# A state-space layer and a routed expert layer on one core: one more GpSimd drain ahead of the last four scatters

## The reference

```python
x = hidden_states                                   # (4, 512, 256)
x = x + state_space_block_and_mlp(_layernorm(x))    # 8 heads, chunks of 128, INTER = 704

# mixture of experts on the 2048 rows of _layernorm(x)
router_probs = softmax(x_flat @ gate_w)             # E = 8
topk_w, topk_idx = top_k(router_probs, 2)
topk_w = topk_w / topk_w.sum(-1, keepdims=True)
h   = silu(x_sorted @ w1[e]) * (x_sorted @ w3[e])   # M = 896, rows sorted by expert
out = (h @ w2[e])                                   # back to token order, weighted by topk_w
x = x + out
```

## Time and profile before

| what | us |
|---|---|
| median of the runs shown | 771.83 |
| lowest of the runs shown | 770.54 |
| span of the profiled execution | 770.9 |
| PE busy in it | 722.1 |
| DVE busy | 605.0 |
| POOL busy | 248.7 |
| ACT busy | 241.7 |

### The profile page before, as it was taken

The page is one execution under the profiler, slowest core; times in us unless marked ns, Lnnn a source line. Parts: engine busy times, 40 slices in busy tenths (PEclk is TensorE's granted clock), DMA queues, the critical chain, the costliest instruction groups (busy, mean ns, idle before and its releaser), DMA issues.

```text
span 770.9 us, 10269 instructions
## 1 busy us (share of the span) xinstructions
PE 722.1 (94%) x2835; PEld 472.6 (61%) x2836; DVE 605.0 (78%) x1452; ACT 241.7 (31%) x486; POOL 248.7 (32%) x404
## 2 busy tenths in 40 slices
PE   6888889999999999999879999999999999999993
PEld 4355665568566755857836666666666666666662
DVE  3899989788965854677829888888888888888881
ACT  1576647674586273231011111111111111111110
POOL 2134422533241532200032333334434333333322
PEclk9999979999999999999999999999999999999997
DMA  9123002000400090050059911111111111111111
GB/s 323 45 98 111 0 1 94 17 1 0 138 28 0 28 314 0 29 171 28 28 171 307 313 27 27 27 28 27 27 29 32 28 33 27 27 27 27 27 14 20
DMA packets 31437, 52.10 MB, mean 68 GB/s; under 512 B 3216, under 2 KB 23120, under 8 KB 31408
## 3 DMA queue, kind: packets, MB, share of 16 engines
q1 hardware_dynamic: 23920, 41.51, 15.6%
q0 software_dynamic: 7488, 10.23, 7.9%
HBM read 42.10 MB, written 9.63 MB: 67 GB/s over the span
## 4 chain that ended last, share of the span: by engine, by line
PE 74%; DVE 14%; issue 3%; POOL 3%; ACT 2%; DMA 2%; DVEq 0%; POOLq 0%; ACTq 0%
PE ps L1035 29%; PE ps L1047 14%; PE ps L715 4%; PE ps L727 4%; PE ps L741 4%; PE ps L409 3%; PE ps L464 3%; PE ps L531 2%; DVE big L1559 2%; PE ps L681 2%; DVE big L1579 2%; PE ps L588 2%; PE ps L478 2%; DVE big L2113 2%; DVE big L1590 1%
## 5 line engine op out<-in xcount | busy, mean ns | idle before, releaser
L2113 DVE STREAM_TRANSPOSE big<-big 32x224 f32<-32x224 f32 x608 | 244.8, 403 | 9.1
L1035 PE MATMUL ps<-big 128*128 x624 | 242.8, 542 | 1.1 <-ACT big L1461 1.1
L1035 PEld LDWEIGHTS ps<-big 128*128 128x128 f32 x624 | 119.0, 191 | 106.0 <-issue 104.1
L1047 PE MATMUL ps<-big 128*128 x546 | 124.5, 380 | 1.1 <-DVE big L2113 0.7
L1047 PEld LDWEIGHTS ps<-big 128*128 128x128 f32 x546 | 100.8, 190 | 14.0 <-issue 1.9
L2160 POOL TENSOR_TENSOR big<-big 128x1 f32<-128x1 f32 x115 | 41.0, 356 | 206.6 <-DVE big L2122 186.2
L1467 ACT ACTIVATE big<-ps 128x896 f32<-128x896 f32 x39 | 35.8, 917 | 217.3 <-PE ps L1035 217.3
L2129 DVE TENSOR_TENSOR big<-big,ps 128x896 f32<-128x896 f32 x39 | 42.4, 1088 | 49.3 <-PE ps L1035 49.2
L2357 POOL DMA_INDIRECT out_rows<-big x39 | 62.7, 1608 | 22.7 <-issue 22.7
L409 PEld LDWEIGHTS ps<-big 128*128 128x128 f32 x325 | 41.3, 146 | 40.0 <-issue 26.4
L409 PE MATMUL ps<-big 128*128 128x128 f32 x325 | 53.6, 280 | 9.9 <-ACT big L1098 2.3
(11 more groups left out here) (180 smaller groups left out, 915.5 us busy)
## 6 DMA issues: line engine op xcount, KB each, us to landing
big<-in_w SPq DMA_DIRECT2D x24, 896.0 KB, 7.4
big<-cum_rows SPq DMA_DIRECT2D x16, 512.0 KB, 5.3
out_rows<-big SPq DMA_DIRECT2D x4, 512.0 KB, 2.9
xn_rows<-big SPq DMA_DIRECT2D x4, 512.0 KB, 3.2
big<-in_hidden SPq DMA_DIRECT2D x1, 1536.0 KB, 12.0
big<-in_in_proj SPq DMA_DIRECT2D x1, 1288.0 KB, 7.0
big<-in_gate SPq DMA_DIRECT2D x1, 640.0 KB, 12.9
big<-in_up SPq DMA_DIRECT2D x1, 640.0 KB, 8.7
```

What stands on the lines that cost most here:

```text
L1035: last = mm(bank(bk + n)[:, 0:HALF], xT[:, k, :], expert_cols(e, off + k * M + n * HALF, HALF), start=(k == 0), stop=(k == KD - 1))
L1047: last = mm(bank(7)[:, 0:D], hTs[:, half, j * P:(j + 1) * P], expert_cols(e, 2 * KD * M + j * D, D), start=(j == 0), stop=(j == MB - 1))
L2113: last = V.transpose(hTs[c * SQ:(c + 1) * SQ, half, :].rearrange("p (j t) -> p j t", j=MB)[:, :, q * SQ:(q + 1) * SQ], ha[q * SQ:(q + 1) * ...
```

## The change

One instruction is added to POOL: a drain between the loop and the last four scatters. No other instruction changes its place on any engine, and no wait on a semaphore is added or removed.

```diff
                     pass_wait(7)
                     gather(i + 4, 1 - odd)
                     add_rows(i, 1 - odd)
+            G.drain()
             for i in range(TILES - 4, TILES):
                 add_rows(i, i % 2)
             g.wait_ge(y_added, 16 * TILES)
```

## The result

| | median us | lowest to highest | ratio to the kernel before |
|---|---|---|---|
| before, beside the first sample, 6 runs | 772.0 | 770.30 to 776.33, and one at 1942.74 | |
| before, beside the second sample, 23 runs | 772.1 | 768.68 to 776.90 | |
| before, beside the third sample, 29 runs | 771.86 | 765.42 to 776.67 | |
| changed, first sample, 6 runs | 763.03 | 759.22 to 767.22 | 0.990 (0.987 to 0.993) |
| changed, second sample, 6 runs | 765.44 | 761.29 to 769.49 | 0.990 (0.986 to 0.994) |

The forecast was 765.5 us and a gain of 6.06 us, which is a ratio of 0.992. It lies in the interval of each sample; weighted by their runs the three ratios average 0.992. The run of 1942.74 us is left out of the ratios. As a time, the first sample's median, 763.03 us, lies under the forecast's own range (from 764.2) and under the wide one (from 763.8); the other two medians lie inside both.

A forecast was written before the change was run, and what follows sets the result against it. PE's matmuls were taken to bound the body, leaving POOL's tail: 770.9 us less 6.06 at the closing drain, added drain free, gives 764.8 profiled. Timed runs were forecast at 765.5 us, own range 764.2 to 766.9, wide range 763.8 to 772.2.

The forecast's parts named there:

- the wide one: Range for the timed runs meant to hold 8 in 10, taking in the no-effect cases: 763.8 to 772.2 us.
- What bounds the kernel: Whole program: PE busy 722.1 of 770.9 us sets the body; only POOL's work after PE's end can be shortened.
- The price per indirect DMA: POOL's closing drain: 6438 ns read as bookkeeping over 78 gathers and scatters, 82.5 ns for each.
- The added drain: Behind scatter 34 on POOL: 74 DMAs take 6.1 us, scatter 35 comes 0.2 to 2.3 us late, cost 0.
- The early case: Added drain works from scatter 34's end on POOL, records in order, and ends at 740.65 us.
- The late case: Added drain first waits for every landing, ends at 742.8 us; scatter 35 comes at 744.4.
- The cover: POOL's 6.57 us idle before tile 35's small add hides the drain; scatter 35 has 4.7 us in hand.
- The closing drain: POOL's drain at the program's end finds four scatters, takes 0.38 us instead of 6.44, saving 6.06 us.
- The sum: Profiled span: 770.9 - 6.06 = 764.8 us; timed runs taken as 765.5 us.
- Fixed price: Rival: any drain behind indirect DMAs costs 6.44 us or walks all records again; no effect, 771.8 us in runs; chance 0.22.
- empty drain: Rival: the added drain only passes, the closing 6.44 us belong to the program's end; 771.8 us in runs; chance 0.07.
- Slower, the walk runs beside DVE: Rival: DVE's transposes stretch the added drain to 23.5 us, delaying the last scatters; 780.0 us, 1.2% slower; chance 0.04.

The follow-up runs named there:

- third sample: The changed kernel timed again, twelve runs on another chip than the second sample, against the kernel before: 766.42 us, ratio 0.993 (0.990 to 0.997).
- the place without it: The added drain moved between scatter 37 and scatter 38, against the kernel before: ratio 0.996 (0.994 to 0.998).
- The pairs of executions with a like start: Profiles of kernel before, changed, changed again and small add in the drain's place, paired by TensorE's granted clock: spans 770.9 and 765.2, 766.6 and 760.7 us.
- the second drain: Two drains one behind the other instead of the changed kernel's one; one timed run, 764.16 us.
- 17 turns: A drain at the end of each of the loop's 17 turns and none behind the loop, against the kernel before: ratio 0.993 (0.990 to 0.996).

## Why the prediction was right

*What bounds the kernel.* The reading held: PE and its body are as they were (342.4 us from first to last scatter), and the gain comes from what POOL does after its last scatter has landed. One reading is off: the chain leaves PE at 742.13 us and not at 749.96, with DVE's multiply and transposes ahead of the weighing. No term of the sum rests on it.

*The price per indirect DMA.* It was 82.5 ns from a single row. The experiments give the drain by its records: 47 ns with none, 135 with one, 380 with four, 6099 with 74, 6438 with 78. From none to four this is (380 - 47) / 4 = 83 ns, from 4 to 78 it is (6438 - 380) / 74 = 82 ns. The straight line of the prediction stands, through gathers and scatters alike. Two things stay open: what POOL does in this time ("records" and "walk" are names for a time that grows with the number of DMAs; no row shows the work), and whether the price goes by the DMA or by its rows, since all 78 move 128 rows.

*The added drain.* Forecast 6.1 us behind the end of scatter 34, measured 6.12. The early case held: the walk starts with the records whose data has long landed, and scatter 34, landed by then, is last. The late case (all landings first) is out: scatter 34 landed at 732.3 in this trace, and 6.1 us behind that is 738.4, not 736.2.

*The cover.* Scatter 35 was to be 0.2 us late and is 0.02 us late against scatter 34, because its index copy takes 0.18 us on a free POOL and not the 0.73 assumed. That the cover is what makes the drain free is shown by the place without it, where 4.4 us are exposed.

*The closing drain.* Forecast 0.38 us and a saving of 6.06; measured 380 ns and 6.06 us.

*The sum.* The profiled span was to be 764.8 and is 760.7. The step that missed is the one that carries the profiled execution over to another execution: it took the state of the kernel up to the tiles as given, and that moved by 4.4 us. The pairs of executions with a like start give 5.7 and 5.9 us. For the timed runs the term that was too small is their spread, 1.3 us, taken from two runs of the kernel before (771.83 and 770.54); twelve runs of it spread over 10 us, and so the first sample's median could fall under the range. That 24 runs of the changed kernel average 765.4 us, beside a forecast of 765.5, is closer than such a spread lets one forecast, and in part luck. The upper end of the forecast's range, 766.9, does not follow from the terms that it names: 771.83 - 5.8 is 766.0. Nor does little lie around the span, as was read from the kernel before: in every run that has both, the time is 1.7 to 1.9 us above its own span. The sum is not hurt by it, since it takes a difference.

*The rivals.* "Fixed price" falls with the second drain's 47 ns, and "empty drain" with the closing drain's 380 and the added one's 6.12 us. "Slower, the walk runs beside DVE" falls too: 74 records beside DVE's transposes take 6.12 us, and 74 with no engine busy at the program's end take 6.10. The stretch of the added drain in the changed kernel, columns as above, has DVE busy for 8.01 of 9.20 us:

```profile
728.40:737.60 9.20, 9.20 (x34) 5.82 (x33) 8.01 (x18) 1.30 (x2) 1.99 (x3) 1.00 0.13 14
```

## What to carry to other kernels

Look at what lies between the last busy instruction and the end of the span, by the source line of the program's end; the chain of waits does not show it. Where GpSimd has issued many indirect DMAs, its closing drain can cost time for each of them, here some 82 ns for a DMA of 128 rows, and a drain placed in an earlier idle stretch of GpSimd takes that work off the end. It must stand where the idle time covers it, and here one was enough.

## What was not expected of the hardware

A POOL drain does two things: it waits until the data of the indirect DMAs issued before it has landed (it ended 0.20 us behind the last landing in 16 of 17 turns), and it spends 82 ns on each one since the last drain even if all have long landed. Two executions of one program were up to 10 us apart here, with a lead that, in the traces, arises ahead of the tiles and goes with the stretches in which TensorE is granted 1.2 GHz; a gain of 6 us could be read exactly from the closing drain's row of any one trace, and only roughly from the times.
